# Graph attention in four layers: the adjacency loaded by casting DMAs from GpSimd's queue, folded on VectorE and packed in 16 slices

## What is computed

```python
h = x @ W                                  # 4 heads of 64 columns
s_src, s_dst = h . a1, h . a2              # one score per node and head
e = leaky_relu(s_src[i] + s_dst[j], slope) # slope 0.01 in layer 0, 0.2 in layer 1
e = where(adj[i, j] == 0, -inf, e)
out[i] = sum_j softmax_j(e)[i, j] * h[j]
```

## Time and profile before

| | |
|---|---|
| median of 3 runs | 2997.62 us (2996.97 to 2999.9) |
| the profiled execution | 2995.74 us; its span, from the first to the last instruction, 2993.9 us |
| mean granted TensorE clock | 0.994 of full speed |
| TensorE busy | 2923.0 us, 98% |
| VectorE busy | 2133.9 us, 71% |
| ScalarE busy | 1920.6 us, 64% |
| GpSimd busy | 1179.6 us, 39% |
| adjacency loads | 64 issues on SP's queue, 1024 KB each, 4.9 us to landing (median) |

### The profile page before, as it was taken

How to read it: one execution, slowest core, us unless ns; L and a number is a source line. 1 busy time by engine, 2 the same in 40 slices (tenths; PEclk the granted TensorE clock), 3 DMA queues, 4 the chain that set the end, 5 groups by cost and what they waited for, 6 DMA issues and landing times.

```text
span 2993.9 us, 65253 instructions
## 1 busy us (share of the span) xinstructions
PE 2923.0 (98%) x24628; PEld 2556.9 (85%) x24628; DVE 2133.9 (71%) x3887; ACT 1920.6 (64%) x3414; POOL 1179.6 (39%) x1559
## 2 busy tenths in 40 slices
PE   7999999999989999999999999999999999989999
PEld 6899999999979999999998878887788878755555
DVE  5999898888888888888896556566666656562245
ACT  4777999999988999999985545444455444430000
POOL 0672385641226565654121023333323333444222
PEclk9999999999999999999999999999999999999999
DMA  8677100000100000000010000000000000000001
GB/s 292 207 234 246 39 11 15 11 11 14 62 15 13 11 15 11 15 11 15 11 35 12 4 1 4 4 1 4 1 4 4 1 1 1 3 1 1 0 14 42
DMA packets 41912, 104.55 MB, mean 35 GB/s; under 512 B 9856, under 2 KB 23424, under 8 KB 33536
## 3 DMA queue, kind: packets, MB, share of 16 engines
q1 hardware_dynamic: 39616, 101.61, 10.4%
q10 hardware_dynamic: 2112, 0.52, 0.1%
HBM read 97.73 MB, written 4.39 MB: 34 GB/s over the span
## 4 chain that ended last, share of the span: by engine, by line
PE 89%; DVE 5%; ACT 2%; issue 2%; DMA 1%; POOL 1%; SPq 0%; DVEq 0%; POOLq 0%; ACTq 0%
PE bank L1377 21%; PE bank L1380 21%; PE bank L1435 16%; PE bank L1473 13%; PE bank L1383 11%; PE bank L1308 2%; PE bank L1462 2%; DMA arena<-in_adj_dram 1%; PE bank L1449 1%; DVE rings L1804 1%; DVE arena L1724 1%; PE bank L1320 1%; ACT above L974 1%; PE bank L1358 1%; DVE rings L1799 1%
## 5 line engine op out<-in xcount | busy, mean ns | idle before, releaser
L1377 PE MATMUL bank<-values,rings 128*128 128x195 bf16 x8192 | 1392.1, 248 | 31.5 <-DVE rings L1807 19.0
L1380 PE MATMUL bank<-values,rings 128*128 128x195 bf16 x8192 | 1392.0, 248 | 0.0
L974 ACT ACTIVATE above<-srow,kpass 128x512 fp8e4<-128x512 f32 x2032 | 1279.9, 709 | 96.2 <-DVE rings L1807 87.1
L1377 PEld LDWEIGHTS bank<-values,rings 128*128 128x128 fp8e4 x8192 | 802.9, 98 | 44.0 <-issue 39.8
L1380 PEld LDWEIGHTS bank<-values,rings 128*128 128x128 fp8e4 x8192 | 802.9, 98 | 0.4
L1804 DVE TENSOR_TENSOR rings<-rings,above 128x512 uint32<-128x512 uint32 x512 | 387.1, 756 | 171.8 <-PE bank L1380 135.4
L1062 ACT ACTIVATE values<-srow,cmul 128x512 f32<-128x512 f32 x256 | 206.0, 815 | 411.5 <-PE bank L1473 410.5
L1807 DVE TENSOR_TENSOR rings<-rings 128x512 uint32<-128x512 uint32 x512 | 425.7, 831 | 17.3
L1473 PE MATMUL bank<-hv,values 128*128 128x257 f32 x1792 | 420.6, 380 | 0.0
L1473 PEld LDWEIGHTS bank<-hv,values 128*128 128x128 f32 x1792 | 335.0, 190 | 69.9 <-issue 25.2
L1383 PE MATMUL bank<-values,rings 128*128 128x390 bf16 x1920 | 318.7, 329 | 10.1 <-DVE values L1840 10.1
(11 more groups left out here) (223 smaller groups left out, 3483.5 us busy)
## 6 DMA issues: line engine op xcount, KB each, us to landing
arena<-in_adj_dram SPq DMA_DIRECT2D x64, 1024.0 KB, 4.9
srow<-src_dram SPq DMA_DIRECT2D x69, 256.0 KB, 3.1
x<-in_x_dram SPq DMA_DIRECT2D x4, 1024.0 KB, 11.4
out_dram<-x SPq DMA_DIRECT2D x7, 512.0 KB, 2.9
arena<-in_L_gnn_fe_w_dram SPq DMA_DIRECT2D x2, 512.0 KB, 7.2
arena<-in_L_gnn_W_hz_dram SPq DMA_DIRECT2D x1, 1024.0 KB, 7.7
arena<-in_L_gnn_g_w_dram SPq DMA_DIRECT2D x1, 1024.0 KB, 10.9
weights<-in_L_gnn_W_dram SPq DMA_DIRECT2D x3, 256.0 KB, 3.5
```

Of the source, the lines that this page charges most:

```text
L974: last = act.activation(above[:, k % 2, q, :], srow[:, par, :], ACT.Relu, scale=BIG, bias=kpass[:, p % 2, k * Q + q:k * Q + q + 1], satura ...
L1377: pe.matmul(acc[:, 0:KW], pos[:, k % 2, q, :].bitcast(FP8)[:, rows], v[:, 0:KW], start=start, stop=final, skip_group_check=True)
L1380: last = pe.matmul(acc[:, KP:KP + KW], neg[:, k % 2, q, :].bitcast(FP8)[:, rows], v[:, KP:KP + KW], start=False, stop=final, skip_group_ch ...
```

## The change

- The adjacency is loaded by one DMA for each tile from GpSimd's queue into bf16 buffers, so the transfer turns int32 into bf16. Three buffers (`STAGED`) instead of two halves; the load of tile `t` waits until tile `t - 3` is folded. The first ten are issued after half of `x` has landed, the others in `front()`, between values and quotients.
- `convert(t, 0)` makes the left half of a tile 0 or 1 and the right half 0 or 16, both in place; `convert(t, 1)` adds them. TensorE then packs 16 slices with the powers 1, 2, 4 and 8.
- 8 tiles are loaded and packed first, 6 of them woven. The first half of tile 7's fold stands in the statistics, the second in the first unit. A tile is packed as a whole after units 2, 4 and 6.
- `FRONT` has (0, 4) ahead of (1, 0). The values of pass 1 begin during the first group, with `quot` as scratch, in another order, two chunks for each of four groups, and TensorE waits for them unit by unit (`made`).
- In layers 0 and 1 the scores of the last quad are computed by matmuls of their own ahead of its dense products (`scores_first`), copied at once, and the statistics wait for them alone. Only the first unit's masks are made ahead; the second's come after the first chunk of values. The first chunk takes the second exponential's values first and waits for each exponential by itself.

```diff
-PACKED_FIRST = 7
+PACKED_FIRST = 8
-PACKED_WOVEN = 5
+PACKED_WOVEN = 6
-FRONT = [(0, 0), (0, 1), (0, 2), (0, 3), (1, 0), (0, 4), (0, 5), (1, 1), (0, 6), (0, 7)]
+FRONT = [(0, 0), (0, 1), (0, 2), (0, 3), (0, 4), (1, 0), (0, 5), (1, 1), (0, 6), (0, 7)]
+VALUES_ORDER = [0, 3, 1, 2, 4, 5, 6, 7]
+VALUES_MADE = [max(VALUES_ORDER.index(j) for j in range(k + 1)) + 1 for k in range(BITS)]
+STAGED = 3
...
-        adj_in = arena[:, 0:4096].bitcast(I32).rearrange("p (s n) -> p s n", s=2)
-        adj_bf = arena[:, 4096:8192].bitcast(BF16).rearrange("p (t s n) -> p t s n", t=2, s=2)
+        adj_in = arena[:, 0:6144].bitcast(BF16).rearrange("p (s n) -> p s n", s=STAGED)
+        adj_bf = arena[:, 6144:8192].bitcast(BF16).rearrange("p (t n) -> p t n", t=2)
...
+            def load_adj(t):
+
+                if t >= STAGED:
+                    pool.wait_ge(s_adjbf, t - STAGED + 1)
+                pool.dma_start(adj_in[:, t % STAGED, :], A["adj"][t * P:(t + 1) * P, :])\
+                    .then_inc(s_adj[t % STAGED], 16)
+
+            pool.wait_ge(s_x[1], 16)
+            for t in range(PACKED_FIRST + STAGED - 1):
+                load_adj(t)
...
             def front():
 
-                values = {0: (0, 1, 2), 1: (3, 4, 5), 2: (6, 7)}
-                for at, (p, g) in enumerate(FRONT[:-1]):
-                    for v in values.get(at, ()):
-                        values_of(0, 1, v)
+                values = {at: VALUES_ORDER[2 * at:2 * at + 2] for at in range(NG // 2)}
+                load_adj(PACKED_FIRST + STAGED - 1)
+                for at in range(len(FRONT)):
+                    vtmp = vtmp_pool if at else quot
+                    loads = [t + STAGED for t in packs_of(at) if t + STAGED < T]
+                    order = values.get(at, ())
+                    for t in loads[:1 if at < 2 else 2]:
+                        load_adj(t)
+                    if at < 2:
+                        values_of(0, 1, order[0], vtmp)
+                        for t in loads[1:2]:
+                            load_adj(t)
+                    if at > 0:
+                        quotient(0, *FRONT[at - 1], (at - 1) % 2, at - 1)
+                    for t in loads[2:]:
+                        load_adj(t)
+                    for v in order[1 if at < 2 else 0:]:
+                        values_of(0, 1, v, vtmp)
...
+            def scores_first(l, q, tiles):
+
+                if l == 0:
+                    pe.wait_ge(s_packed, (PACKED_WOVEN - 1) // 2 * 2 + 1 + CREDIT)
+                for i in tiles:
+                    pe.wait_ge(s_xt, q * 2 + (l * 2 * QUADS + i // 2 + 1))
+                    for k in range(2):
+                        last = pe.matmul(bank[6][:, i * 2 * H:(i + 1) * 2 * H], xT[q % 2][:, i, k, :],
+                                         weights[:, k, F:F + 2 * H], start=(i == 0 and k == 0),
+                                         stop=(i == QT - 1 and k == 1), skip_group_check=True)
...
             def pack_half(t, half, b):
 
-                pe.wait_ge(s_adjbf, t * 2 + half + 1)
-                for k in range(half * (BITS // 2), (half + 1) * (BITS // 2)):
+                pe.wait_ge(s_adjbf, t + 1)
+                for k in range(half * (BITS // 4), (half + 1) * (BITS // 4)):
...
-                    if 1 <= k <= 2 * len(packs):
+                    if k in (2, 4, 6) and k <= 2 * len(packs):
...
-                        if (p, g) == (1, 0):
-                            pe.wait_ge(s_vals, NG)
...
             def convert(t, half):
 
-                dve.wait_ge(s_adj[half], (t + 1) * 16)
+                raw = adj_in[:, t % STAGED, :]
+                if half == 0:
+                    dve.wait_ge(s_adj[t % STAGED], (t // STAGED + 1) * 16)
+                    dve.tensor_scalar(raw[:, 0:N // 2], raw[:, 0:N // 2], 0.0, None, ALU.is_gt)
+                    dve.tensor_scalar(raw[:, N // 2:], raw[:, N // 2:], 0.0, float(2 ** (BITS // 2)),
+                                      ALU.is_gt, ALU.mult).then_inc(s_adjone, 1)
+                    return
                 if t >= 2:
-                    dve.wait_ge(s_packmm, t * 2 + half - 3 + CREDIT)
-                dve.tensor_scalar(adj_bf[:, t % 2, half, :], adj_in[:, half, :], 0, None, ALU.is_gt)\
+                    dve.wait_ge(s_packmm, t * 2 - 2 + CREDIT)
+                dve.wait_ge(s_adjone, t + 1)
+                dve.tensor_tensor(adj_bf[:, t % 2, :], raw[:, 0:N // 2], raw[:, N // 2:], ALU.add)\
                     .then_inc(s_adjbf, 1)
...
-                for k in range(UNITS_AHEAD):
-                    for _ in masks(l, TURN[l] * H * UNITS + k, k, packed[:, :, 0:WORDS]):
-                        pass
+                for _ in masks(l, TURN[l] * H * UNITS, 0, packed[:, :, 0:WORDS]):
+                    pass
...
-                    dve.wait_ge(s_h, T * (l + 1) + 1)
+                    dve.wait_ge(s_h, T * l + (T - QT + 1))
+                    dve.wait_ge(s_lastscores, l + 1)
...
                     shifted.then_inc(s_shift, 1)
-                    dve.wait_ge(s_exps, l + 1)
+                    if l == 0:
+                        convert(PACKED_FIRST - 1, 0)
+                    dve.wait_ge(s_expone, l + 1)
...
                     if l == 0 and first and k == 0:
-                        store_packed(PACKED_WOVEN, 6 + PACKED_WOVEN % 2)
+                        convert(PACKED_FIRST - 1, 1)
...
                             first_rests(l, 0)
                             first_lasts(l, 0)
+                            for _ in masks(l, unit + 1, 1, words):
+                                pass
+                            if l == 0:
+                                store_packed(PACKED_WOVEN, 6 + PACKED_WOVEN % 2)
```

88 lines of the change are left out of this document (54 added, 34 removed).

## The result

The changed kernel takes **3004.35 us** (median of 13 runs, 3000.56 to 3005.47) against 2998.29 us for the kernel before on the same chip (13 runs, 2996.58 to 3000.16). The ratio is 1.0019, with a 95% interval of 1.0012 to 1.0027: slower by 6 us, where 8.4 us less were forecast. The profiled execution took 3004.37 us, its span is 3002.5 us (before: 2995.74 and 2993.9).

The account below looks back on a forecast made before the run. Bounds: DMA and TensorE nearly together in loading, VectorE in groups 0 to 3, TensorE in groups 4 to 9. Terms: 0.0 up to group 4, -9.4 for groups 4 to 8, +1.0 layer 1: -8.4, so 2989 us; range 2979 to 3006.

Parts of the forecast that it names:

- Loading stage: Loads before the first product: 5.8 us a tile, first product at 64.5 us against 68.5, -4.0 us.
- Price of the fold: VectorE's fold per tile: 0.69 us per scalar operation, 1.22 for the addition, the low end; 2.35 start to start.
- The new addition is disturbed as well: Groups 4 to 7: disturbance also slows the addition on VectorE, 0.3 us within 25.0 us a group.
- The stall of 2.39 at group 3 goes: Start of group 3: the wait for a stored pack vanishes, one more tile being packed by then, -2.4 us.
- Groups 0 to 3: VectorE-bound stage after the first product: +2.9, +1.0, -2.4 and +2.5, so +4.0 us.
- Groups 4 to 7: VectorE is late next at 25.0 us a group; each group gives 1.9 us, -7.6 in all.
- the sign of a wrong forecast: The forecast is wrong if groups 5 to 7 stay above 26 us.
- Layer 1: Layer 1's start: 0.5 us gained by sooner scores, 1.5 lost by the second unit's masks, +1.0 us.
- rival 1: Adjacency loads: the cast slows the transfer, 11.5 us a tile, groups follow the DMA; 3070 us, chance 0.13.
- rival 2: Fold on VectorE: the addition goes by columns, one more microsecond per tile; 3018 us, chance 0.07.
- rival 3: Groups 4 and 5: GpSimd comes late with the loads, 3 to 4 us lost each; 2996 us, chance 0.13.
- rival 4: Loading stage: DMA keeps its 6.55 us a tile, hiding the gain, groups still win 1.9 each; 2994 us, chance 0.12.

Follow-up runs that it names:

- the last experiment: Variant with one tile in three folded from group 5 on and changed starts (2981.4 us), second head's first group at place 4, not 5: 2977.98 us.
- the narrow one: Changed kernel with the additions of the 24 tiles folded inside the groups made over 256 of 2048 columns: 2985.13 us, ratio 0.9953.

## Why the prediction was wrong

The measured 3004.35 us lies in the stated range, 2979 to 3006, but by luck: that end of the range stood for loads that come late, which didn't happen, and faster by 8.4 became slower by 6.

- **Loading stage, right in number and lucky.** -4.3 for -4.0. The transfer is quicker than forecast (5.12 us a tile, not 5.8), so tile 7, which was to set the first product, didn't. GpSimd's late maximum did, and took back what the loads had won.
- **Price of the fold, right, and its cost misplaced.** 0.69, 0.69 and 1.22 us are the low end exactly. "The new addition is disturbed as well" is wrong: it stays at 1.22 us, the comparisons stretch. The fold's extra cost on VectorE in groups 0 to 3 (4.7 us, tile 7's addition taken off) is somewhat above the 3.5 forecast.
- **"The stall of 2.39 at group 3 goes", wrong.** It moved to group 4 with 1.88 us. With one tile more packed ahead but (0, 4) ahead of (1, 0), the group at place 4 needs the twentieth tile, the last one packed in the group before. The order of `FRONT` could have told that; the last experiment shows it.
- **Groups 0 to 3, mis-sized.** +11.5 for +4.0. The forecast gave VectorE 6.4 us more work (2.9, 2.5 and 1.0) and 2.4 less idle time. It got 9.5 us more work (above all the fold 4.7, masks 3.6, tile 7's addition 1.2) and 2.0 us more idle time: the stall that didn't go, and a wait of 2.21 for a TensorE that had starved in group 0 and come back at a lower clock. The sum had no term for that wait. Without the additions, and with GpSimd's values later, groups 0 to 4 were 15.8 us shorter.
- **Groups 4 to 7, the step that failed.** +0.2 for -7.6. The prediction let a group take the larger of the engines' sums, 25.0. Groups 5 to 7 take 26.8, the sign of a wrong forecast that it had named (above 26). The sums were right (24.35 and 24.9 busy). But the addition and the sums of banks fall into units 1 to 5, where VectorE takes 3.4 to 3.9 us against TensorE's 2.7 to 3.6, and its room in units 6 and 7 is closed by the two mask buffers: there it waits for TensorE. The series of none, one, two and three additions (26.9, 26.0, 26.25, 26.8) and the narrow one (24.3) show the addition as the cause; ScalarE's queue is 0.33 us of it. That the unevenness, and not the sum with its small gaps, closes the last microsecond was not separated: the six operations were never spread otherwise.
- **Layer 1, mis-sized.** +2.4 for +1.0. Some 1.7 stand at its start (531.1 against 529.4, as above): the moved masks and 1.9 us of score matmuls, for scores that come no sooner than the exponentials can use them. The other 0.7 weren't traced, nor was 1.0 us behind layer 1.
- **Rivals.** The cast slows nothing (rival 1), the addition takes 1.22 us and not 2.3 (rival 2), no group waits for a load or a value (rival 3), and the loads come faster, not as before (rival 4). The rival that happened was missing: work moved from TensorE, busy all the time, to VectorE, busy nearly so.

On the two pages: the Trainium skill, "VectorE: DVE Perf Modes", section "The perf-mode tier table", gives 693 and 1224 ns for these operations, and the undisturbed ones in the trace agree to 10 ns. The Trainium skill's page "SBUF — State Buffer", section "Who interferes with whom", has GpSimd's descriptor writing locked out by VectorE's two-port modes. No row here shows work that waits for a load behind the first product: each issue takes 0.53 to 0.86 us on GpSimd, and what it waits for is the fold. From issue to landing a load takes 7.9 to 12.0 us in the groups, and whether a part of that is the lock isn't shown.

## What to carry to other kernels

Where one engine is busy throughout and another nearly so, don't add the work up over the stage: lay it out unit by unit, with the buffers between them, and see in which units the second engine becomes the last. The same work has another price beside other work: among the groups, additions gained time only in the quiet ones, where GpSimd does little. A change of several parts can hide a gain in its loss: here everything but the additions in the groups is worth 12 us together, and those additions ate 18. A DMA issue that waits stands in its engine's queue: look at what small, urgent instruction comes behind it, which here began another 6 to 9 us after the issue.

And one profiled execution is one sample: the same group 0 took 35.8 to 38.0 us.

## What had not been expected of the hardware

- A DMA that turns int32 into bf16 went faster than the plain loads: 2 MB read in 5.12 us, 410 GB/s of source bytes with three in flight, against 339 GB/s before. How much of that is the longer queue was not separated.
- Beside GpSimd's elementwise work the comparison of 2048 bf16 columns stretches from 0.69 us to as much as 1.15, the addition of the same columns not at all (1216 ns on average in groups 0 to 3, 1214 in the quiet groups).
- GpSimd's maximum over the partitions begins 6.4 to 7.1 us after the last casting load ahead of it is issued (8.7 in one run), with nothing in the profile that it waits for. In the kernel before, where GpSimd issues no loads, it begins 0.14 us after its input is there. The cause is open.
